# Six layers on one core: the hand-overs between the first five dealt out in parts

## The reference

```python
x = x + L0_xattn(ln(x), ctx)   # cross attention, 16 heads, output projection
x = x + L0_attn(ln(x))         # causal attention, 16 heads, biases, projection
x = x + L0_ffn(ln(x))          # 256 -> 1024 -> 256, quantised weights and activations
x = x + L1_xattn(ln(x), ctx)   # q = x Wq + bq; softmax(q (ctx Wk + bk)^T) (ctx Wv + bv), one head
x = x + L1_attn(ln(x))         # causal attention, 16 heads
x = x + L1_ffn(ln(x))          # 32 routed experts (8 of them per token) and a shared one
```

## Time and profile before

| | |
|---|---|
| median of 3 runs | 1286.99 us (1286.65 to 1287.81) |
| the profiled execution: time | 1285.13 us |
| its span in the trace | 1283.0 us |
| PE, DVE, ACT, POOL busy | 93%, 63%, 50%, 44% of the span |
| mean granted clock of TensorE | 0.989 |
| chain that ended last, by engine | PE 79%, DVE 7%, issue 5%, ACT 5%, POOL 4% |

### The profile page before, as it was taken

The page is one execution under the profiler, slowest core; times in us unless marked ns, Lnnn a source line. Parts: engine busy times, 40 slices in busy tenths (PEclk is TensorE's granted clock), DMA queues, the critical chain, the costliest instruction groups (busy, mean ns, idle before and its releaser), DMA issues.

```text
span 1283.0 us, 30312 instructions
## 1 busy us (share of the span) xinstructions
PE 1197.6 (93%) x9820; PEld 946.3 (74%) x9828; DVE 810.0 (63%) x1773; ACT 643.5 (50%) x1394; POOL 558.5 (44%) x833
## 2 busy tenths in 40 slices
PE   6899999989997777998998999999999999999998
PEld 5677777767775445877776888888888888888886
DVE  4688888757776885658999875444444544444444
ACT  5766666634454786545556443334334433343342
POOL 2244444467775443548887433333233223323322
PEclk9999999989999998999999999999999999999999
DMA  8200000000000000210000133333333343333331
GB/s 286 59 18 16 16 16 8 2 1 2 0 0 18 16 0 10 74 30 14 1 0 1 54 108 120 114 110 106 109 103 114 121 128 103 110 114 114 105 112 62
DMA packets 34041, 80.13 MB, mean 62 GB/s; under 512 B 4416, under 2 KB 12096, under 8 KB 33984
## 3 DMA queue, kind: packets, MB, share of 16 engines
q1 hardware_dynamic: 32800, 78.09, 18.7%
q10 hardware_dynamic: 1184, 1.31, 0.3%
HBM read 77.03 MB, written 2.36 MB: 62 GB/s over the span
## 4 chain that ended last, share of the span: by engine, by line
PE 79%; DVE 7%; issue 5%; ACT 5%; POOL 4%; DMA 0%; ACTq 0%; DVEq 0%; POOLq 0%; SPq 0%
PE ps L2117 10%; PE ps L2119 10%; PE ps L2118 10%; PE ps L2200 5%; PE ps L2199 5%; PE ps L2201 5%; PE ps L421 4%; PE ps L968 3%; PE ps L436 3%; PE ps L409 3%; PE ps L959 2%; PE ps L938 2%; PE ps L975 2%; PE ps L947 2%; POOL Sm L1212 1%
## 5 line engine op out<-in xcount | busy, mean ns | idle before, releaser
L2486 POOL TENSOR_TENSOR sw<-sg,wb 128x512 f32<-128x512 f32 x136 | 176.4, 1297 | 386.7 <-ACT sg L2310 352.8
L2389 DVE TENSOR_TENSOR a<-sw,ps 128x512 f32<-128x512 f32 x136 | 93.5, 687 | 224.8 <-POOL sw L2486 224.5
L2315 ACT ACTIVATE ah<-a 128x512 fp32r<-128x512 f32 x136 | 86.0, 632 | 290.7 <-DVE a L2389 268.5
L2117 PE MATMUL ps<-Hh,wh 128*128 128x512 f32 x544 | 215.3, 396 | 0.0
L2118 PE MATMUL ps<-Hl,wh 128*128 128x512 f32 x544 | 214.4, 394 | 0.0
L2119 PE MATMUL ps<-Hh,wl 128*128 128x512 f32 x544 | 214.4, 394 | 0.0
L2393 DVE TENSOR_TENSOR al<-a,ah 128x512 fp32r<-128x512 f32 x136 | 95.5, 702 | 62.5 <-ACT ah L2315 59.3
L674 ACT ACTIVATE Pr<-ps,mx 128x256 f32<-128x256 f32 x256 | 103.9, 479 | 61.1 <-DVE mx L575 61.1
L2119 PEld LDWEIGHTS ps<-Hh,wl 128*128 128x128 f32 x544 | 101.8, 187 | 25.1
L2117 PEld LDWEIGHTS ps<-Hh,wh 128*128 128x128 f32 x544 | 101.9, 187 | 24.8 <-issue 0.8
L2118 PEld LDWEIGHTS ps<-Hl,wh 128*128 128x128 f32 x544 | 101.9, 187 | 23.6
(11 more groups left out here) (238 smaller groups left out, 2469.1 us busy)
## 6 DMA issues: line engine op xcount, KB each, us to landing
wb<-token_weights SPq DMA_DIRECT2D x64, 512.0 KB, 3.7
raw<-in_ew SPq DMA_DIRECT2D x66, 384.0 KB, 3.0
cT<-in_ctxT SPq DMA_DIRECT2D x16, 256.0 KB, 2.7
cx<-in_ctxT SPq DMA_DIRECT2D x15, 256.0 KB, 2.7
X<-in_x SPq DMA_DIRECT2D x1, 1536.0 KB, 7.2
wqkv<-in_wqkv SPq DMA_DIRECT2D x2, 768.0 KB, 5.1
raw3g<-in_wg SPq DMA_DIRECT2D x1, 1024.0 KB, 5.5
raw3u<-in_wu SPq DMA_DIRECT2D x1, 1024.0 KB, 7.6
```

The costliest lines, as they stand in the source:

```text
L2117: eng.matmul(ps[:, bank, :], wh[:, u, w], HhT[:, c, cols], start=(c == 0), stop=False)
L2389: eng.tensor_tensor(a[:, tt, :], sw[:, tt, :], ps[:, UB[tt], :], ALU.mult).then_inc(m_a, 1)
L2486: eng.tensor_tensor(sw[:, tt, :], sg[:, tt, :], wb[:, u, tt * UT:(tt + 1) * UT], ALU.mult).then_inc(m_sw, 1)
```

## The change

Every hand-over is dealt out: a layer's opening and its close are each cut into parts, and `in_turn` lays them alternately. The new `in_turn` issues this layer up to its mark TAIL, then part 1 of the next opening, part 1 of the close, part 2 of the opening, and so on; what is left of either side follows.

```diff
+MAIN, TAIL, PART = "main", "tail", "part"
 def in_turn(eng, *layers):
     programs = [layer(eng) for layer in layers]
-    next(programs[0])
+    while next(programs[0]) != MAIN:
+        pass
     for this, following in zip(programs, programs[1:]):
-        next(this)
-        next(following)
+        while next(this) != TAIL:
+            pass
+        mark = next(following)
         for _ in this:
-            pass
+            if mark != MAIN:
+                mark = next(following)
+        while mark != MAIN:
+            mark = next(following)
```

**The close of cross_heads** (the others' engines are cut at the same places):

```diff
@@ cross_heads, tensor
+        def finish():
+            i, u, v = NPAIR - 1, 1, 0
+            mix(i - 1, v, 2)
+            turn(i - 1, 7)
+            yield TAIL
+            turn(i, 0)
...
+            turn(i, 3)
+            mix(i, u, 0)
+            yield PART
+            turn(i, 4)
+            mix(i, u, 1)
+            tail2(i - 1, v)
+            turn(i, 5)
+            tail3(i - 1, v)
+            turn(i, 6)
+            yield PART
+            mix(i, u, 2)
+            turn(i, 7)
+            yield PART
+            mix(i, u, 3)
+            mixed(i)
+            yield PART
+            tail2(i, u)
+            tail3(i, u)
@@ cross_heads, gpsimd
+        def finish():
+            for t in range(NPAIR - 3, NPAIR):
+                quantise(t)
+            yield TAIL
```

**The opening and the close of self_heads.** The first scores of pair 0 and the projection of pair 1 move from the first regular pass into the opening. The opening serves layer 2 and layer 5, the close layer 2 alone:

```diff
@@ self_heads, tensor
+        def first():
+            if layer == 2:
+                eng.wait_ge(s_w1, late)
+                eng.wait_ge(g["c_ke"], 2 * NPAIR)
+                eng.wait_ge(g["c_ve"], 2 * NPAIR)
+            else:
+                eng.wait_ge(g["d_qe"], 2 * NPAIR)
+            ln_pe(eng, L, 0, 0, F0)
+            yield PART
+            if layer == 5:
+                eng.wait_ge(g["d_ce"], NPAIR)
+            qkproj(0, 0)
+            yield PART
+            if layer == 2:
+                eng.wait_ge(g["c_exp"], 8 * NPAIR - 1)
+            else:
+                eng.wait_ge(ln_hT, g["lnt"][3] + NPAIR)
+            vproj(0, 0)
+            yield PART
+            if layer == 2:
+                eng.wait_ge(g["c_exp"], 8 * NPAIR)
+            ln_pe(eng, L, 1, 1, FH)
+            yield PART
+            if layer == 5:
+                eng.wait_ge(g["d_exp"], NPAIR)
+            scores(0, 0, 0)
+            qkproj(1, 1)
@@ self_heads, scalar
+        def first():
+            eng.wait_ge(s_w1, late)
+            eng.wait_ge(g["s_bq"], 2)
+            ln_act(eng, L, 0, 0, F0)
+            yield PART
+            qk_out(0, 0)
+            yield PART
+            ln_act(eng, L, 1, 1, FH)
@@ self_heads, tensor
+        def finish():
+            i, u, v = NPAIR - 1, 1, 0
+            scores(i, u, 0)
+            turn(i - 1, v, 1)
+            yield TAIL
+            pv(i - 1, v, 1)
+            scores(i, u, 1)
+            yield PART
+            turn(i, u, 0)
+            tail2(i - 1, v)
+            pv(i, u, 0)
+            tail3(i - 1, v)
+            turn(i, u, 1)
+            yield PART
+            pv(i, u, 1)
+            tail2(i, u)
+            tail3(i, u)
```

**The feed-forward** opens with `xt(0)`, then the second half of gate and up, then the first half (`gate(0, 0, 1)`, `up(0, 0, 1)`; `gate(0, 0, 0)`, `up(0, 0, 0)`). The weight product that was `setup` stands in its first regular pass, and the last `down` moves one pass later:

```diff
@@ quantised_ffn, tensor
         def body(i, u):
+            if isinstance(i, int) and i == 0:
+                eng.wait_ge(g["a_te"], 2 + 2 * NPAIR)
+                eng.wait_ge(g["a_on"], NPAIR)
+                g["turn_weights"](eng, AT)
             if front:
                 xt(i + 1, v)
                 gate(i + 1, v, 0)
...
-            if tail:
+            if within(i, 1, last):
                 down(i - 1, v)
+            elif isinstance(i, int) and i == last + 2:
+                down(last, u)
+            if isinstance(i, int) and i == 0:
+                g["weight_product"](eng, AT)
@@ quantised_ffn, scalar
+        def first():
+            xt_out(0, 0)
+            yield PART
+            silu(0, 0, 0)
+            yield PART
+            silu(0, 0, 1)
```

**cross_single** opens with the passes -3 and -2 (the norm of pair 0) as one part and the pass -1 (the norm of pair 1, `qproj(0)`) as the next, without `setup`. Its close is cut in five:

```diff
@@ cross_single, tensor
+        def finish(body):
+            scores(last, 1, last % R, last // R)
+            mix(last - 2, 1)
+            yield TAIL
+            keys(last, last % R)
+            turn(last - 1, 0)
+            vproj(last - 2, 1)
+            yield PART
+            body(NPAIR, 0, NPAIR // R)
+            yield PART
+            yield PART
+            mix(last, 1)
+            yield PART
+            vproj(last, 1)
@@ cross_single, scalar
+        def finish(body):
+            turned(last - 1, 0)
+            yield TAIL
+            mixed(last - 2, 1)
+            exps(last, 1)
+            yield PART
+            mixed(last - 1, 0)
+            turned(last, 1)
+            yield PART
+            mixed(last, 1)
```

More of the change, by code:

```diff
@@ L554, in body @@
                 scores(i + 1, v, 0)
+        def finish():
[4 more added lines that the diff above has]
+            turn(i, 0)
+            mix(i - 1, v, 3)
+            turn(i, 1)
+            mixed(i - 1)
+            turn(i, 2)
+            scores(i, u, 1)
[17 more added lines that the diff above has]
+            tail3(i, u)
         def weight_sums():
@@ L1136, in vector @@
                                         row=row)
-        yield from pipeline(eng, body)
+        if proj:
+            yield from long_pipeline(eng, body, first=first, finish=finish)
+        else:
+            yield from routed_pipeline(eng, body, first)
     def scalar(eng):
@@ L1257, in body, with first, finish @@
                 g["wb_ones"](eng)
+        def first():
+            ln_pool(eng, L, 1, 1)
+            yield PART
+            spread(0, 0, 0)
+            spread(0, 0, 1)
+        def finish():
+            i, u, v = NPAIR - 1, 1, 0
+            yield TAIL
+            residual(i - 1, v)
+            centre(i, 0)
+            yield PART
+            centre(i, 1)
+            residual(i, u)
         if not proj:
             g["tail5"]["gpsimd"] = dict(next_scale=next_scale)
-        yield from pipeline(eng, body)
+        if proj:
+            yield from long_pipeline(eng, body, first=first, finish=finish)
+        else:
+            yield from routed_pipeline(eng, body, first)
     return {"tensor": tensor, "vector": vector, "scalar": scalar, "gpsimd": gpsimd}
@@ L1302, in within, with pairs @@
         return not isinstance(i, int) or low <= i <= high
-    def pairs(eng, body):
-        for i in range(-2, 0):
-            body(i, i % 2)
-        yield
+    def pairs(eng, body, first):
+        yield from first()
+        yield MAIN
         for i in range(0, 2):
@@ L1315, in pairs @@
             body(i, i % 2)
-        yield
-        for i in range(NPAIR, NPAIR + 2):
-            body(i, i % 2)
+        yield TAIL
+        body(NPAIR, 0)
+        yield PART
+        body(NPAIR + 1, 1)
     last = NPAIR - 1
@@ L1443, in body, with first @@
                 ln_dve(eng, L + 1, 0, v)
-        yield from pairs(eng, body)
+        def first():
+            front1(0, 0)
+            ln_dve(eng, L, 1, 1)
+            yield PART
+            ln_dve2(eng, L, 1, 1, f_r)
+            front1(1, 1)
+            ln_dve(eng, L, 2, 0)
+        yield from pairs(eng, body, first)
     def scalar(eng):
@@ L1494, in body, with first @@
                 round2(i, u)
-        yield from pairs(eng, body)
+            if isinstance(i, int) and i == 0:
+                g["weight_product_out"](eng, AT)
+        def first():
+            xt_out(0, 0)
+            yield PART
+            silu(0, 0, 0)
+            yield PART
+            silu(0, 0, 1)
+        yield from pairs(eng, body, first)
     def gpsimd(eng):
@@ L1534, in body, with first @@
                 scales(i + 2, u)
-        yield from pairs(eng, body)
+        def first():
+            round1(0, 0)
+            scales(0, 0)
+            yield PART
+            ln_pool(eng, L, 1, 1)
+            yield PART
+            round1(1, 1)
+            scales(1, 1)
+        yield from pairs(eng, body, first)
     return {"tensor": tensor, "vector": vector, "scalar": scalar, "gpsimd": gpsimd}
```

327 lines of the change are left out of this document (217 added, 110 removed).

## The result

The changed kernel takes 1273.2 us (median of 5 executions, 1269.69 to 1273.65) against 1287.68 before (median of 5): a ratio of 0.9875, 95% interval 0.9854 to 0.9897. It saves 14.5 us, where 18.3 were forecast. The profiled execution is the quickest of the five, 1269.69 us with a span of 1267.7, against 1285.13 and 1283.0: 15.3 us of span to find.

A forecast was written before the change was run, and what follows sets the result against it. PE was taken to bound the attention stages, DVE the feed-forward. Savings of 6.2 + 1.7 + 8.6 + 1.8 = 18.3 us took the profiled 1285.13 to 1266.8; with 1.86 for the median, 1268.7 us, range 1263.5 to 1278.

The forecast's parts named there:

- Hand-over 1: From cross_heads to causal 2: turn 1 of pair 0 at 278.7 instead of 284.89, 6.2 us saved; bounds 3 and 8.7.
- Hand-over 2: From causal 2 to the feed-forward: `mul(0)` at 412.2 instead of 413.89, 1.7 us saved; bounds -1 and 3.
- copied 402.75: End of causal 2: ACT's `xt_out(0)`, behind exponentials ready at 402.3, is copied at 402.75; turn 0 loses 1.3 us.
- The clock of 1.00 in all four windows: Named sign of being right: PE's granted clock is 1.00 in the windows over all four hand-overs.
- It fell in all four: Argument for the rival of a falling clock: in the earlier trace the clock fell in every hand-over.
- Hand-over 3: From the feed-forward to cross_single: first scores 8.1 us sooner, next pass 0.5 quicker, 8.6 us saved; bounds 5 and 9.5.
- The sum by that rule, 5.2: Feed-forward to cross_single: if transposes don't engage full rate, the slow stretch stays and 5.2 us is saved, not 8.6.
- Hand-over 4: From cross_single to layer 5: turn 1 of pair 0 at 580.7 instead of 582.52, 1.8 us saved; bounds 0 and 3.2.
- a wait above 1 us that I hadn't named: Named sign of error: PE shows a wait longer than 1 us that the prediction didn't list.
- The product had its cover: Feed-forward's first pass: weight product delays nothing, cover 1.3 us on ACT; `mul(1)` later than 4.8 us behind `mul(0)` would be wrong.
- the clock falls again: Rival: the low clock returns in the first and third hand-overs, costing 8.5 us: 1277.2 us; chance 0.16.
- waits move to the heads of the queues: Rival: a 0.56 us wait at each of PE's 15 inserted parts, 8.4 us, 2.3 counted: 1274.8 us; chance 0.17.

The follow-up runs named there:

- wait filled: The changed kernel with 14 unused transposes added on PE in the wait ahead of the feed-forward's first gate: 1269.48 us, ratio 0.9863.
- product late: The changed kernel with only the weight product put back to the head of cross_single's opening: 1275.56 us, ratio 0.9895.
- quantise late: The changed kernel with only `quantise` steps 14 and 15 put back behind pair 0's `spread` on POOL: 1272.51 us, ratio 0.9891.
- hand-over 1 undone: The changed kernel with cross_heads closed undealt and causal 2 opened in one piece ahead of it, as before: 1278.64 us, ratio 0.9915.
- mask first: The changed kernel with `mask(0, 1)` ahead of the second half of pair 2's norm on DVE, causal 2 and layer 5: 1267.91 us, ratio 0.9844.

## Why the prediction was right, and where it was not

The sign, the range and the two large terms held; the time was 4.5 us above the forecast, point by point:

- **Hand-over 1**, 6.2 forecast, 6.06 measured (5.55 by undoing it). The clock held, the wait ahead of turn 1 of pair 0 was 1.09 for 1.2. `quantise` 15 ended at 261.6 (forecast 259.8) and cost nothing; put back it costs 2.2 in A-B. `mask(0, 1)` came 0.75 us later than forecast, 0.6 of it from the start-up.
- **Hand-over 2**, 1.7 forecast, -0.39 measured. This is the step that failed. The order is worth 1.27. The step "copied 402.75" had the wait too small, 1.3 us for 1.8 to 2.2: exponentials in front of a copy aren't only their own time on ACT, they hold it until POOL releases them (ACT stands 1.98 us for POOL there). And in or behind that wait the clock fell in 5 of 7 profiles, for 1.4 to 2.6 us: 1.27 less the 1.66 of the first profile is the -0.39. I had weighed such falls for hand-overs 1 and 3 only, and priced a wait that I had named myself at its length alone. The clock of 1.00 in all four windows, named as a sign of being right, failed here with 0.87. "It fell in all four" was misread as well: the low clock in the second of the earlier trace rows lies from 420 us on, behind this hand-over.
- **Hand-over 3**, 8.6 forecast, 8.94 measured, at clock 1.00: 4.4 the product (5.5 by PE's and ACT's rows together, as the experiment expected), 4.5 the dealing with the fall that went, which no run separates. The Trainium skill (TensorE: Matmul & The Clock Gate, Part 4: PE-mode transpose) says that full rate doesn't engage for transposes. Here it did: the 8 transposes of `at(15)` took 1.09 us with the granted clock at 1.00, and in "wait filled" 14 in a row took 1.75 us at full clock. The sum by that rule, 5.2, is out. In this hand-over the clock did fall in 3 of the other 10 dealt-out profiles, by 1.6, so its 1.00 was likely and not certain.
- **Hand-over 4**, 1.8 forecast, 1.39 between the traces, and this was right for a wrong reason: undone at full clock it is 0.18 quicker. My sum compared a new order at full clock with a trace that held a fall. The wait of 1.57 ahead of turn 1 was the named sign of error (a wait above 1 us that I hadn't named).
- **From the profile to the median.** I added 1.86 us, what before showed. The changed kernel's was 3.5: its profiled execution, the quickest of its five, had falls in no hand-over but the second; its repeat had another one in hand-over 4, and took 1271.74 us. Of eleven executions one is at 1267.9 us, one at 1269.7, three from 1271.3 to 1271.7 and six from 1273.0 to 1273.7. Steps of this size go with the 1.6 that a fall cost in hand-over 3 or 4; that each step is one was not shown beyond the profiles.

The product had its cover: `mul(1)` came 4.77 us behind `mul(0)`, as needed (but see "product late" for the pass behind it). Of the rivals, "the clock falls again" was the mechanism that cost most, in other hand-overs than it named, and "waits move to the heads of the queues" was what set it off in 2 and 4. Why the same wait is followed by a fall in one execution and not in the next stays open.

## What to carry over

When parts of one stage are dealt into another, look at what stands in front of each inserted part's operand on the engine that makes it: moving `xt_out`, `mask(0, 1)` and `mask(15, 0)` was worth 7 us, half as much as the whole change, and about half of that shows in the order itself. Price an idle PE of 1.6 us and more inside busy work above its length (here the clock fell with it in 10 of 15 cases, for 1.4 to 2.6 us more), and compare orders at equal clocks, stretch by stretch, before crediting one with a microsecond or two.

## What was not expected of the hardware

The same program keeps 2.4 GHz behind a wait in one execution and not in another: with a wait of 1.57 us ahead of turn 1 in hand-over 4, the projection behind it took 1.95 us in the changed kernel's first profile and 3.57 in its second. It is so across kernels that are alike in the stretch, too: with the gate's wait at 2.03 to 2.04 us, B-C takes 120.25 (product late, quantise late) or 122.9 (hand-over 1 undone, mask first). And a fall costs nothing where PE isn't what the others wait for: product late has one from 412 to 417 us (clock 0.66), and its C-D is 72.66 all the same.
